# Four chained layers on one Trainium2 core: the second normalisation's transposes taken from TensorE to VectorE squares and DMA, and the last layer run two steps behind

## The chip, the core and the metric

The program runs on one core of one Trainium2 chip. The metric is the device time of the whole program in microseconds (us), median of the runs shown. The engines of the core run their own instruction streams side by side and wait for each other on semaphores: TensorE (PE in the rows, PEld its weight loads), VectorE (DVE), ScalarE (ACT), GpSimd (POOL) and SyncE (SP, which here only issues DMAs).

## The reference

Four layers, each added to the running x, over 2 sequences of 2048 tokens with 512 features:

```python
x = x + L0(x)   # gates, exponential averages, LayerNorm
x = x + einsum('bti,bio->bto', x, W[cat]) + b                      # L1
h = relu(einsum('bsh,bha->bsa', x, w1) + b1)                        # L2: 512 -> 128 -> 512
y = x + einsum('bsa,bah->bsh', h, w2) + b2
x = x + (y - mean(y)) * rsqrt(var(y) + 1e-5) * gamma + beta
x = x + einsum('bnh,boh->bno', x, W3[subj]) + b3                    # L3
```

The change touches nothing of L0. It is about L1, L2 and L3, which the program runs in its second part.

## The kernel before

The tokens are cut into 8 blocks of 512 tokens (NBLK = 8, LAST = 7), 4 blocks to a sequence (PER_SEQ = 4). The first part, to about 475 us of the trace, computes L0 for all blocks and keeps its results in DRAM (n_scratch, xt_scratch). The second part runs one step for each block i, in which L1 and the first half of L2 are done for block i and the rest for block i-1.

Every fp32 product is made of three passes: the operands are split in a high and a low part (x_h and x_l, s_h and s_l, t_h and t_l), and high by high, low by high and high by low are added up in PSUM (L628 to L630). The parts are made by two engines: ScalarE writes the high one and VectorE subtracts it for the low one. Within a product the features lie on the partitions. LayerNorm needs tokens on the partitions. So a block changes its layout twice in a step:

- `xx_product` (L867) brings x2, the result of L1, to tokens with four 128x128 transposes (L635, `turn`) and adds the L2 product to it in PSUM bank pm[k], for the token tile k;
- VectorE takes the statistics (`norm2_stats`, L1659), GpSimd makes scale and shift (`norm_scale`), ScalarE and VectorE each normalise two of the four tiles into stage_a (L1273, L1669);
- `turn_n2` (L882) brings the normalised block n2 back to features with 16 more transposes, in the middle of the next step's L1 product;
- `x3_sum_part` (L1633) makes gamma * n2 + (x2 + beta) from PSUM, `x3_hi_part` (L1257) and `x3_lo_part` (L1642) split it into t_h and t_l, and the L3 product (`l3_tile`, L911) uses them in the same step. ScalarE had made x2 + beta into soma (`x2_beta`, L1251).

The order of a step on TensorE is: L1 chunk 0, half of chunk 1, turn_n2 of two chunks, the rest of chunk 1, half of chunk 2, turn_n2 of two chunks, the rest, chunk 3, (in steps 5 and 6 also four turns of the next L1 input, `turn_y`), L3 tile 0, the first L2 product (`w1_product`), L3 tiles 1 and 2, the four `xx_product`, L3 tile 3. L1, L3 and w1 chunks are 12 matmuls of 512 columns each. L1 chunks alternate between two PSUM banks, so chunk 2 waits until ScalarE and VectorE have read chunk 0, and chunk 3 until they have read chunk 1 (`l1_product`, L833).

SyncE loads the next block's inputs (`load_y`, L417) and stores each output tile from one of two buffers in x_tok (`store_out`, L427); `output` (L1652) on VectorE waits for the store that last used its buffer. Steps 2, 3, 5 and 6 run in loops, steps 1, 4 and 7 are written out.

## Time and profile before

| | us |
|---|---|
| median of 3 runs (lowest, highest) | 754.29 (753.92, 754.69) |
| the profiled execution | 753.31 |
| its span, first to last instruction | 751.4 |
| TensorE busy in the span | 742.9 |
| VectorE, ScalarE, GpSimd busy | 536.7, 364.8, 113.2 |

The granted TensorE clock is 1.00 over the span. 1.9 us of the profiled execution lie outside the span, and the median is 1.0 us above that execution. Matmuls overlap in the rows: one of 512 columns is shown as 0.39 us long while the next begins 0.23 us after it, so what one costs is read from the distance of two beginnings.

### The profile page before, as it was taken

Reading aid. Unit: us, or ns where it says so; the run is one execution under the profiler, and the core shown is the slowest. Engines: PE = TensorE matmul, PEld = TensorE weight load, DVE = VectorE, ACT = ScalarE, POOL = GpSimd, SP = SyncE. Lnnn points to the kernel's source line nnn. Section 1 sums busy time; section 2 is a strip of 40 time slices with the busy share of each in tenths; the row PEclk is TensorE's granted clock in tenths of the full one; section 3 lists DMA queues with packets and bytes.
Section 4 is the critical chain, followed back from the end, with each engine's and each line's share of the span. In section 5 each row is a group of like instructions: output and inputs, shape, how many; then the busy total and the mean of one; then the engine's idle time right before and its main releaser. Section 6 shows DMA issues by size and latency. Waiting matters only on the chain.

```text
span 751.4 us, 10452 instructions
## 1 busy us (share of the span) xinstructions
PE 742.9 (99%) x3421; PEld 605.6 (81%) x3421; DVE 536.7 (71%) x790; ACT 364.8 (49%) x546; POOL 113.2 (15%) x222
## 2 busy tenths in 40 slices
PE   7999999999999999999999999999999999999997
PEld 6888888888888888788888788888888888888885
DVE  5598895695695595596587589866877767666645
ACT  4373346445436535535535543656563553635331
POOL 2000040030022013004004024124301021010110
PEclk9999999999999999999999999999999999999999
DMA  8863008916934953962971872526144131331002
GB/s 263 227 188 38 28 1 117 189 59 103 187 73 82 190 92 69 185 109 56 169 138 34 135 223 83 197 85 224 58 153 150 46 127 57 127 113 68 28 35 79
DMA packets 93068, 86.17 MB, mean 115 GB/s; under 512 B 61631, under 2 KB 75998, under 8 KB 90990
## 3 DMA queue, kind: packets, MB, share of 16 engines
q1 hardware_dynamic: 91662, 81.57, 45.4%
q10 hardware_dynamic: 1184, 4.23, 1.6%
q8 instruction: 15, 0.25, 0.1%
q0 software_dynamic: 192, 0.00, 0.1%
q14 instruction: 15, 0.12, 0.1%
HBM read 33.33 MB, written 25.20 MB: 78 GB/s over the span
## 4 chain that ended last, share of the span: by engine, by line
PE 98%; DVE 1%; DMA 0%; issue 0%; ACT 0%; DVEq 0%; ACTq 0%
PE pc L630 13%; PE pc L628 13%; PE pc L629 13%; PE pm L628 6%; PE pm L629 6%; PE pm L630 6%; PE pt L628 6%; PE pt L630 6%; PE pt L629 6%; PE pm L747 4%; PE pm L746 4%; PE pm L745 4%; PE pm L635 3%; PE pt L635 3%; PE pm L877 1%; PE pm L878 1%
## 5 line engine op out<-in xcount | busy, mean ns | idle before, releaser
L628 PE MATMUL pc<-x_h,wg_h 128*128 128x512 f32 x224 | 88.5, 395 | 0.1
L630 PE MATMUL pc<-x_h,wg_l 128*128 128x512 f32 x224 | 88.0, 393 | 0.0
L629 PE MATMUL pc<-x_l,wg_h 128*128 128x512 f32 x224 | 87.7, 391 | 0.0
L1443 DVE TENSOR_TENSOR_SCAN stage_b<-alpha,carry,stage_b 128x512 f32<-128x512 f32 x64 | 78.4, 1267 | 0.0
L628 PE MATMUL pm<-wo_h,s_h 128*128 128x512 f32 x128 | 50.7, 396 | 0.0
L1119 ACT ACTIVATE ctx_t<-ctx_t,col_all 128x512 f32<-128x512 f32 x32 | 23.1, 723 | 56.6 <-DVE ctx_t L1423 56.6
L630 PE MATMUL pm<-wo_h,s_l 128*128 128x512 f32 x128 | 50.5, 395 | 0.0
L629 PE MATMUL pm<-wo_l,s_h 128*128 128x512 f32 x128 | 50.5, 395 | 0.0
L747 PE MATMUL pm<-t_h,wt_l 128*128 128x512 f32 x128 | 50.5, 395 | 0.0
L746 PE MATMUL pm<-t_l,wt_h 128*128 128x512 f32 x128 | 50.4, 394 | 0.0
L745 PE MATMUL pm<-t_h,wt_h 128*128 128x512 f32 x128 | 50.4, 394 | 0.0
L628 PEld LDWEIGHTS pc<-x_h,wg_h 128*128 128x128 f32 x224 | 42.1, 188 | 10.2 <-issue 1.2
L630 PEld LDWEIGHTS pc<-x_h,wg_l 128*128 128x128 f32 x224 | 42.1, 188 | 9.3
L629 PEld LDWEIGHTS pc<-x_l,wg_h 128*128 128x128 f32 x224 | 42.1, 188 | 9.1
L1396 DVE SCALAR_TENSOR_TENSOR gate<-gate,soma 128x512 f32<-128x512 f32 x32 | 21.9, 697 | 36.7 <-ACT gate L1074 36.6
L522 POOL TENSOR_TENSOR newton<-mv,const 128x4 f32<-128x4 f32 x16 | 9.6, 600 | 251.0 <-DVE mv L1664 180.9
L1437 DVE SCALAR_TENSOR_TENSOR stage_b<-mod,w_blend,ctx_t 128x512 f32<-128x512 f32 x64 | 45.6, 754 | 2.4 <-DVE ctx_t L1427 1.5
L1074 ACT ACTIVATE gate<-pm,col_all 128x512 f32<-128x512 f32 x32 | 21.6, 688 | 45.4 <-PE pm L747 30.9
L1125 ACT ACTIVATE t_h<-stage_b 128x512 fp32r<-128x512 f32 x32 | 20.4, 637 | 47.5 <-DVE stage_b L1450 47.4
L1273 ACT ACTIVATE stage_a<-pm,nbias,rstd 128x512 f32<-128x512 f32 x16 | 11.6, 774 | 55.9 <-POOL nbias L538 55.8
L1630 DVE SCALAR_TENSOR_TENSOR s_l<-pc,seq_b,s_h 128x512 fp32r<-128x512 f32 x28 | 21.0, 750 | 24.0 <-ACT x_t L1248 24.0
L630 PE MATMUL pc<-x_h,ws_l 128*128 128x512 f32 x96 | 38.0, 395 | 0.0
(248 smaller groups left out, 1932.3 us busy)
## 6 DMA issues: line engine op xcount, KB each, us to landing
x_planes<-x_pairs SPq DMA_DIRECT2D x52, 256.0 KB, 7.4
xt_scratch<-x_t SPq DMA_DIRECT2D x8, 1024.0 KB, 10.2
n_scratch<-stage_a SPq DMA_DIRECT2D x8, 1024.0 KB, 10.1
ctx_t<-xt_scratch SPq DMA_DIRECT2D x16, 512.0 KB, 6.6
x_pairs<-n_scratch SPq DMA_DIRECT2D x14, 512.0 KB, 5.3
out_dram<-x_tok SPq DMA_DIRECT2D x28, 256.0 KB, 2.0
mod<-mod_scratch ACTq DMA_DIRECT2D x8, 512.0 KB, 3.6
stage_b<-in_L_cond_weight_dram SPq DMA_DIRECT2D x2, 1024.0 KB, 5.6
```

Source lines behind the costliest of these rows:

```text
L628: nc.tensor.matmul(acc, ah, bh, start=start and q == 0, stop=False)
L629: nc.tensor.matmul(acc, ah, bl, start=False, stop=False)
L630: last = nc.tensor.matmul(acc, al, bh, start=False, stop=stop and q == n - 1)
L635: last = nc.tensor.matmul(acc[:, q * P:(q + 1) * P], src, ident[:, :], is_transpose=True, start=(q == 0), stop=stop and (q == 3), skip_gro ...
L745: nc.tensor.matmul(pm[m][:, :], wt_h[:, c, o], t_h[:, c, :], start=(c == 0), stop=False)
L746: nc.tensor.matmul(pm[m][:, :], wt_h[:, c, o], t_l[:, c, :], start=False, stop=False)
L747: last = nc.tensor.matmul(pm[m][:, :], wt_l[:, c, o], t_h[:, c, :], start=False, stop=(c == NC - 1))
L1074: nc.scalar.activation(gate[:, m % 2, :], pm[m][:, :], ACT.Tanh, bias=cols["btemp"][:, m:m + 1], scale=0.5).then_inc(gate_t, 1)
L1119: nc.scalar.activation(ctx_t[:, m, :], ctx_t[:, m, :], ACT.Tanh, bias=cols["bg"][:, m:m + 1], scale=0.5).then_inc(z_t, 1)
L1396: nc.vector.scalar_tensor_tensor(gate[:, m % 2, :], gate[:, m % 2, :], 1.0, soma[:, m, :], ALU.add, ALU.mult).then_inc(s_prod, 1)
L1437: nc.vector.scalar_tensor_tensor(tr[:, m % 2, :], mod[:, d, :], w_blend[:, d, m:m + 1], ctx_t[:, m, :], ALU.mult, ALU.mult).then_inc(prods, 1)
L1443: nc.vector.tensor_tensor_scan(tr[:, m % 2, :], alpha[:, 1 + d:2 + d].to_broadcast([P, BLK]), tr[:, m % 2, :], carry[:, D - d, m:m + 1], A ...
```

## The change

- For blocks 1 to 6 TensorE no longer turns n2. ScalarE normalises all four tiles (not two), VectorE transposes each tile in squares of 32x32 (`turn_squares`) from stage_a into stage_b, and 16 DMAs of 32 partitions and 64 KB each (`move_square`) put the squares where a full transpose has them, in x_planes. ScalarE multiplies by gamma and adds beta while it copies them back to stage_b (`scale_n2`), and `x3_sum_part` adds x2. Blocks 0 and 7 are still turned by TensorE.
- Move issues are SyncE's, except that in blocks 1 and 6 six of the 16 are ScalarE's.
- The L3 product of block j is done in step j+2 and no longer in step j+1. So x2 is kept for a step longer, in x_t and soma by turns, and x2_beta is gone. x3_hi, x3_lo and L3 of block 6 come behind step 7.
- Step 1 has only two L3 tiles, step 2 the other two of block 0. The four turns of the second L3 weight (`turn_l3`) stand around the first and last two xx_products of step 1. Step 3 has its splits in another order on ScalarE and VectorE.
- The second L2 weights are loaded to gate, and VectorE makes their low parts. SyncE issues the loads of blocks 2 and 3 in step 1 and those of block 4 behind the moves of block 1; the later loads stand between the stores of a step, behind its moves. All loops of the second part are written out.

```diff
+        def x2_of(i):
+            return x_t if i % 2 == 0 else soma
+        def x3_parts_of(j):
+            return (s_h, s_l) if j == LAST - 1 else (t_h, t_l)
+        def turned_by_pe(j):
+            return j == 0 or j == LAST
+        def n2_acts(j):
+            return 2 + 4 * j - (2 if j == LAST else 0)
+        squares = stage_b[:, :, :].rearrange("p a e -> p (a e)").rearrange("p (f k i) -> p f k i", k=TILES, i=32)
+        squares_q = stage_b[:, :, :].rearrange("p a e -> p (a e)").rearrange("p (c q r) -> p c q r", c=NC, q=4)
+        def x3_of(j):
+            return x_planes if turned_by_pe(j) else stage_b
...
+        def move_square(engine, q, a):
+            part, tok = slice(32 * a, 32 * a + 32), slice(P * a, P * a + P)
+            engine.dma_start(x_planes[32 * q:32 * q + 32, :, tok], squares_q[part, :, q, :]).then_inc(n2_in, 16)
+        BY_ACT = [(q, a) for q in (2, 3) for a in range(1, 4)]
+        def shares_moves(j):
+            return j == 1 or j == LAST - 1
...
+            def move_n2(j):
+                sp.wait_ge(n2_squares, j * TILES)
+                if j == 1:
+                    sp.wait_ge(x3_lo, NC)
+                else:
+                    sp.wait_ge(n2_scaled, (j - 1) * NC)
+                for q in range(4):
+                    for a in range(4):
+                        if not (shares_moves(j) and (q, a) in BY_ACT):
+                            move_square(sp, q, a)
...
+            for i in range(2, NBLK):
+                move_n2(i - 1)
+                if i == 2:
+                    load_y(4)
+                    store_out(0, 2)
+                    store_out(0, 3)
+                    continue
+                store_out(i - 2, 0)
+                store_out(i - 2, 1)
+                if i + 2 < NBLK:
+                    load_y(i + 2)
+                store_out(i - 2, 2)
+                store_out(i - 2, 3)
+            for j in (LAST - 1, LAST):
                 for k in range(TILES):
                     store_out(j, k)
...
+            def l3_tile(j, k):
+                b = j // PER_SEQ
+                if turns_y(j + 2) and k < 3:
+                    pe.wait_ge(n2_act, n2_acts(j + 1))
+                elif turns_y(j + 2):
+                    pe.wait_ge(y_sum, (j + 3) * NC + 3)
+                elif j == LAST - 1 and k >= 2:
+                    pe.wait_ge(n2_act, n2_acts(LAST))
+                    pe.wait_ge(n2_dve, 4)
+                elif j == LAST - 1 and k == 0:
+                    pe.wait_ge(out_ready, j * TILES - 1)
+                else:
+                    after(pe, out_ready, j * TILES + max(k - 1, 0))
+                ch, cl = x3_parts_of(j)
+                for c in range(NC):
+                    if k == 0:
+                        pe.wait_ge(x3_hi, j * NC + c + 1)
+                        pe.wait_ge(x3_lo, j * NC + c + 1)
+                    last = product(l3_bank(j, k)[:, :], [(ch[:, c, tok], cl[:, c, tok], wh[:, c, :], wl[:, c, :])],
+                                   start=(c == 0), stop=(c == NC - 1))
+                last.then_inc(l3_mm, 1)
...
+            def last_blocks():
+                l3_tile(LAST - 1, 0)
+                l3_tile(LAST - 1, 1)
+                turn_n2(LAST)
+                l3_tile(LAST - 1, 2)
+                l3_tile(LAST - 1, 3)
...
+            def scale_n2(j, m):
+                b = j // PER_SEQ
+                act.wait_ge(n2_in, j * 256)
+                nc.scalar.activation(stage_b[:, m, :].rearrange("p (k a i) -> p k a i", k=TILES, a=4),
+                                     x_planes[:, m, :].rearrange("p (a k i) -> p k a i", k=TILES, a=4), ACT.Identity,
+                                     bias=seq["beta_b2"][:, b, m:m + 1],
+                                     scale=seq["gamma2"][:, b, m:m + 1]).then_inc(n2_scaled, 1)
...
+            def turn_squares(j, k):
+                dve.wait_ge(n2_act, n2_acts(j - 1) + k + 1)
+                if j == 1:
+                    dve.wait_ge(l3_turned, 2 * NC)
+                else:
+                    dve.wait_ge(x3_lo, j * NC)
+                nc.vector.transpose(squares[:, :, k, :], stage_a[:, k, :].rearrange("p (f i) -> p f i", i=32)
+                                    ).then_inc(n2_squares, 1)
...
+            def x3_sum_part(j, m):
+                dve.wait_ge(x2_hi, j * NC + (m + 1))
+                if turned_by_pe(j):
+                    dve.wait_ge(tn_done, (0 if j == 0 else NC) + (m + 1))
+                    after(dve, n2_scaled, 0 if j == 0 else (LAST - 1) * NC)
+                    nc.vector.scalar_tensor_tensor(x_planes[:, m, :], n2_bank(j, m)[:, :],
+                                                   seq["gamma2"][:, j // PER_SEQ, m:m + 1], x2_of(j)[:, m, :],
+                                                   ALU.mult, ALU.add).then_inc(x3_sum, 1)
+                else:
+                    dve.wait_ge(n2_scaled, (j - 1) * NC + (m + 1))
+                    nc.vector.tensor_tensor(stage_b[:, m, :], stage_b[:, m, :], x2_of(j)[:, m, :],
+                                            ALU.add).then_inc(x3_sum, 1)
```

The TensorE order at the end of the program, before: the last L3 tile of block 6, then `turn_n2(LAST)` and the L3 product of block 7.

```order
L630 MATMUL pt<-wt_h,t_l 128x512
L635 MATMUL pc<-ident,stage_a 128x128 [waits n2_dve,n2_act]
L635 MATMUL pc<-ident,stage_a 128x128 x7
L635 MATMUL pt<-ident,stage_a 128x128 [waits out_ready]
L635 MATMUL pt<-ident,stage_a 128x128 x3
L635 MATMUL pt<-ident,stage_a 128x128 [waits out_ready]
L635 MATMUL pt<-ident,stage_a 128x128 x3
L978 MATMUL pm<-wt_h,t_h 128x512 [waits x3_lo,x3_hi]
```

The same place after the change; L682 is `turn`, L675 to L677 are the three passes of `product`, and s_h and s_l are the parts of block 6.

```order
L677 MATMUL pt<-wt_h,s_l 128x512
L682 MATMUL pc<-ident,stage_a 128x128 [waits n2_dve,n2_act]
L682 MATMUL pc<-ident,stage_a 128x128 x7
L682 MATMUL pm<-ident,stage_a 128x128 x8
L675 MATMUL pm<-wt_h,s_h 128x512 [waits n2_dve,n2_act]
```

All four L3 tiles of block 6 come behind step 7 now: two ahead of the turns, two between them and the L3 product of block 7.

VectorE at the beginning of a step in the loop of steps 2 and 3, before: x2_lo (L1630), x3_sum (L1639) and x3_lo (L1645) of the block before, by turns.

```order
L1630 SCALAR_TENSOR_TENSOR s_l<-pc,seq_b,s_h 128x512 [waits x2_hi]
L1634 ISA
L1639 SCALAR_TENSOR_TENSOR gate<-pt,seq_gamma,soma 128x512 [waits x2_all,tn_done]
L1634 REGISTER_ALU
L1639 SCALAR_TENSOR_TENSOR gate<-pt,seq_gamma,soma 128x512 [waits x2_all,tn_done]
L1645 TENSOR_TENSOR t_l<-gate,t_h 128x512 [waits x3_hi,l3_mm] x2
L1628 REGISTER_ALU [waits w1_mm]
L1630 SCALAR_TENSOR_TENSOR s_l<-pc,seq_b,s_h 128x512 [waits x2_hi]
```

VectorE from the end of step 2 into step 3 after the change: x3_sum (L1714) of block 1, then x2_lo (L1700) of block 3, x3_lo (L1727) of block 1, the squares (L1761) of block 2 and y_sum (L1545) of block 4.

```order
L1746 BN_AGGR mv<-stats 128x2 [waits ln2_stats]
L1714 TENSOR_TENSOR stage_b<-stage_b,soma 128x512 [waits n2_scaled,x2_hi] x4
L1700 SCALAR_TENSOR_TENSOR s_l<-pc,seq_b,s_h 128x512 [waits x2_hi,w1_mm]
L1727 TENSOR_TENSOR t_l<-stage_b,t_h 128x512 [waits x3_hi,l3_mm] x4
L1761 STREAM_TRANSPOSE stage_b<-stage_a 128x16x32 [waits x3_lo,n2_act]
L1545 SCALAR_TENSOR_TENSOR ctx_t<-x_pairs,col_all,ctx_t 128x512 [waits yn_in,yx_in]
L1700 SCALAR_TENSOR_TENSOR s_l<-pc,seq_b,s_h 128x512 [waits x2_hi,w1_mm]
```

Between the x2_lo of chunk 0 and that of chunk 1 two x3_lo stood before; now all four, a square transpose and a y_sum stand there.

## Rows read from the trace of the kernel before

**Rows 1.** The page: busy time by engine, and the chain that ended last

```profile
PE 742.9 (99%) x3421; PEld 605.6 (81%) x3421; DVE 536.7 (71%) x790; ACT 364.8 (49%) x546; POOL 113.2 (15%) x222
PE 98%; DVE 1%; DMA 0%; issue 0%; ACT 0%; DVEq 0%; ACTq 0%
```

**Rows 2.** Timeline of PE, step 3: start, length, line, tiles, shape, count

```profile
573.25 0.40 PE L628 MATMUL pc<-x_h,wg_h 128*128 128x512 f32 x1
...
577.16 0.39 PE L630 MATMUL pc<-x_h,wg_l 128*128 128x512 f32 x1
577.39 1.03 PE L635 MATMUL pt<-ident,stage_a 128*128 128x128 f32 x8
578.18 0.48 PE L628 MATMUL pc<-x_h,wg_h 128*128 128x512 f32 x1
578.50 0.39 PE L629 MATMUL pc<-x_l,wg_h 128*128 128x512 f32 x1
...
604.59 0.40 PE L628 MATMUL pc<-x_h,wo_h 128*128 128x512 f32 x1
```

**Rows 3.** Timeline of PE, the end of the program

```profile
733.14 0.39 PE L630 MATMUL pt<-wt_h,t_l 128*128 128x512 f32 x1
733.63 1.06 PE L635 MATMUL pc<-ident,stage_a 128*128 128x128 f32 x8
734.53 1.04 PE L635 MATMUL pt<-ident,stage_a 128*128 128x128 f32 x8
736.72 0.47 PE L978 MATMUL pm<-wt_h,t_h 128*128 128x512 f32 x1 [1.14 <-DVE t_l L1645]
...
747.76 0.40 PE L980 MATMUL pm<-wt_h,t_l 128*128 128x512 f32 x1
```

**Rows 4.** Groups by line and form: busy us, mean ns | idle before

```profile
L1645 DVE TENSOR_TENSOR t_l<-gate,t_h 128x512 fp32r<-128x512 f32 x32 | 22.2, 713 | 2.0 <-ACT t_h L1260 1.1
L1623 DVE SCALAR_TENSOR_TENSOR x_l<-ctx_t,col_all,x_h 128x512 fp32r<-128x512 f32 x32 | 23.3, 760 | 1.4
L1443 DVE TENSOR_TENSOR_SCAN stage_b<-alpha,carry,stage_b 128x512 f32<-128x512 f32 x64 | 78.4, 1267 | 0.0
L1248 ACT ACTIVATE x_t<-pc,seq_b1b 128x512 f32<-128x512 f32 x32 | 21.8, 680 | 0.4 <-PE pm L879 0.4
L1260 ACT ACTIVATE t_h<-gate 128x512 fp32r<-128x512 f32 x32 | 20.2, 633 | 23.3 <-DVE gate L1639 22.9
L1273 ACT ACTIVATE stage_a<-pm,nbias,rstd 128x512 f32<-128x512 f32 x16 | 11.6, 774 | 55.9 <-POOL nbias L538 55.8
```

**Rows 5.** Timelines of VectorE, GpSimd and ScalarE, statistics to normalisation, step 2

```profile
571.49 0.18 DVE L1664 BATCH_NORM_AGGREGATE mv<-stats 128x2 f32<-128x6 f32 x1
...
571.75 0.20 POOL L522 TENSOR_TENSOR newton<-mv,const 128x4 f32<-128x4 f32 x1 [28.82 <-DVE mv L1664]
...
574.63 1.45 ACT L1273 ACTIVATE stage_a<-pm,nbias,rstd 128x512 f32<-128x512 f32 x2 [8.62 <-POOL nbias L538]
```

**Rows 6.** Timelines, step 1: its first PE row, GpSimd's identity add

```profile
511.30 0.40 PE L628 MATMUL pc<-x_h,wg_h 128*128 128x512 f32 x1
...
526.42 3.35 POOL L563 TENSOR_TENSOR stage_b<-stage_b,ident 128x128 f32<-128x128 f32 x4 [5.74 <-DMA stage_b<-in_L_cond_weight_dram]
```

**Rows 7.** DMA issues by line (ns min/median/max) and landing; DMA view, 299.5 to 307.5 us

```profile
L302 SPq DMA_DIRECT2D x_planes<-x_pairs x52: 603/622/1763, 22.9 to 418.0; - x52
DMA to landing us min/median/max: 4.4/7.4/10.2
L429 SPq DMA_DIRECT2D out_dram<-x_tok x28: 332/338/366, 530.1 to 734.3; - x28
L1115 ACTq DMA_DIRECT2D mod<-mod_scratch x8: 345/351/357, 27.0 to 430.8; - x8
...
DMA packets 1088, 1.15 MB, mean 144 GB/s; under 512 B 63, under 2 KB 1074, under 8 KB 1074
q1 hardware_dynamic: 1088, 1.15, 121.4%
```

## What the change was predicted to do, before it was run

> **What bounds the kernel now.** I read the page first: TensorE is busy for 742.9 of 751.4 us, and the chain that ended last is TensorE's for 98% [rows 1]. So time can only be won by taking work from TensorE or by closing its pauses, and it is lost where TensorE newly waits. Next I read TensorE's timeline of one step for what a turn costs [rows 2], then its end of the program, where its last pauses are [rows 3]. The groups by form give what VectorE and ScalarE pay for one 128x512 operation [rows 4], the three timelines of rows 5 the way from statistics to normalised tiles, and the DMA rows what moves inside SBUF cost [rows 7]. The step from 573.25 to 604.59 is 31.34 us long and has no pause in it [rows 2].
>
> **Term 1, the turns that leave.** The matmul before the turn begins at 577.16 and the second one behind it at 578.50, 1.34 us later; two ordinary distances are 0.46 us. Eight transposes cost 0.88 us, a block's sixteen 1.76 us, and six blocks 10.6 us [rows 2]. They lie on the path that sets the end. Products, xx_products and the turns of blocks 0 and 7 stay. A step of 31.34 us becomes 29.6.
>
> **Term 2, the end.** The last L3 tile of block 6 is issued until 733.37 (733.14 + 0.23), sixteen transposes would end at 735.13, and the next product begins at 736.72: 1.6 us of pauses [rows 3]. After the change two L3 tiles (24 matmuls, 5.6 us) stand between the turns and that product, so its wait for x3 goes. What is late next are the statistics of block 7, since VectorE now does x3 of block 6 ahead of them. Counted from the start of step 7: the squares of block 6 are ready at about 11.2 (L1 chunk 3 is being made until 11.0), the moves take 9.3 us (term 4), so they land at 20.5; four scalings and four high parts on ScalarE (eight at 0.63 to 0.68, 5.2 us) end at 25.7, the last low part at 26.4, four statistics with their aggregates at about 1.0 each at 30.4, GpSimd takes 3.0 (571.67 to 574.63) and the two normalisations 1.45 [rows 4, 5]: 34.9. TensorE is at the turns at 29.6 + 5.6 = 35.2. With some ten handings-over between engines, estimated at 0.1 each, a pause of about 0.7 is left: gain 0.9. From the product at 736.72 on, nothing changes (14.7 us to the end of the span).
>
> **Term 3, step 3.** Here the order of VectorE's work makes a new wait. I count from the first matmul of step 3. Before, the last statistics ended 1.2 us after the last xx_product (the aggregate ends at 571.67, the xx_products at 573.25 - 2.80 for an L3 tile = 570.45) [rows 2, 5]. After the change step 3 begins straight behind the xx_products of step 2, so x3_sum of block 1 starts at 1.2 and its four additions end at 4.0 (0.69 each [rows 4]). ScalarE's copy of x2 waits for all four: 4.7. Its low part ends at 5.4, and L1 chunk 2 needs it at 5.5 (24 matmuls at 0.23): just in time. Chunk 3 needs the low part of chunk 1 at 8.3. But in front of it stand: x3_hi of chunks 0 and 1 (to 6.0), ScalarE's two copies of x2 chunk 1 (to 7.3), x3_hi 2 and 3 (to 8.6), VectorE's last x3_lo (9.3), a square (10.0), y_sum (10.7), and the low part itself (11.4). With operations overlapping at their ends, as L1645 does in groups, it is 10.9. So TensorE waits 2.6 to 3.1 us; I take 2.7. In later steps all x3 work is done before chunk 0 is finished (four high parts end at 2.8, chunk 0 at 2.9), the low part of chunk 1 comes at 7.6, and nothing waits.
>
> **Term 4, the moves.** A block's 16 DMAs move 1.05 MB. The trace has no such DMA. The nearest are the four DMAs of 256 KB from x_pairs to x_planes, also inside SBUF, to 64 partitions, in pieces of 1 KB: issues of 0.62 us, landing 7.4 us after the issue, so 9.3 us from the first issue to the last landing for the same bytes [rows 7]. The new pieces are half as long. Lower bound: the issues, 16 at 0.34 (the store's 128 pieces [rows 7]) and 2 us behind, 7.4 us. Upper bound: a piece costs what one of 1 KB does; 1088 packets took 16 engines 8.0 us, 118 ns each, so 2048 would take 15.1 and with issue and landing 16.9 us [rows 7]. I take 9.3, since both carry the same bytes. What it may take: in a step of 29.6 us the squares are ready at 11.5. The moves land at 20.8, the store of output tile 0 is queued behind them and lands at 22.8, output tile 2 waits for its buffer (23.5), the statistics follow (27.1), x3_sum (29.9). It may be 32.5 before the next step's chunks suffer: the limit is 11.9 us, and at the seam, where x3_sum of block 1 has to end at 4.0 of step 3, it is about 12.5. ScalarE's own issues cost it six times 0.35 us [rows 7] in two steps in which it otherwise waits. Cost: 0, with 2.6 us of cover.
>
> The Trainium skill (SBUF, Door 1: The DMA port swizzle) says that 32 partitions reach only 8 of 16 ports and measured 189 GB/s there for 1 MiB. By it alone the data would take 5.5 us and the issues would bound the moves at 7.4, which takes another 0.5 us off the end. The row of DMAs to 64 partitions, 144 GB/s, is below what that page gives for 64 partitions (196), so I keep the row.
>
> **Term 5, the rest.** VectorE gains four squares and loses two normalisations, ScalarE the reverse and four scalings for four x2_beta. A square is an operation of 512 columns: at least 0.69, at most the 1.27 of a scan [rows 4]; I take 0.69. VectorE then works some 24 us of a step of 29.6, and at 1.27 some 26. It adds 0.6 us to term 3 and 1 us elsewhere if it is 1.27. In step 1 TensorE comes to turn_l3 one L3 tile earlier, at 529.9 (511.30 plus 18.6 us of work), and the weights are ready at 529.77 [rows 6]: no pause, with 0.2 us to spare and 0.3 at risk. The second L2 step has one L3 tile (2.8 us) to cover relu and its split, some 2.3 us: 0, or 0.3 if late.
>
> **Sum.** -10.6 - 0.9 + 2.7 = -8.8 us. Span 742.6, its execution 744.5, and against the median 754.29 the forecast is 745.5 us.
>
> **The rivals.**
> A, no new wait in step 3: if x3_sum of block 1 can start earlier or the order costs less than I count, only terms 1 and 2 act: 754.29 - 10.6 - 0.9 to 1.6, 742.1 to 743. For it: the other engines have much free time [rows 1]. Against it: the semaphores leave no other order.
> B, the moves are somewhat late, through slow squares, or since the loads of block 4 run beside ScalarE's last three moves: 12 to 12.9 us in all. Each microsecond over the limit is paid in five steps and once more at the end: 748 to 752.8.
> C, slower: each 512-byte piece costs nearly as much as one of 1 KB. Then the transfer takes the place of the turns as the bound, in every step: 5 x (m - 11.9) + (m - 9.3) us for moves of m us. It breaks even at 13.0 us and at 16.9 costs 33 - 8.8 = 24 us: up to 778. For it: the whole DMA time of the nearest row may be a price per piece, since no row holds the same bytes in other pieces. Against it: nothing shows such a price.
> The Trainium skill (DMA: Bandwidth & Descriptors, Why small descriptors are slow (HBM only)) says that transfers inside SBUF don't suffer from small pieces; by that C falls. No row here shows it.
> D, the change doesn't win what it takes off: TensorE's instructions go, but it waits as long elsewhere. The chain [rows 1] speaks against it.
>
> **How the numbers follow.** Forecast (744.5 to 748) 0.50; A 0.18; B 0.17; within 0.2% of before (D, or C at its break-even) 0.04; C 0.11. 0.2%, 1.5 us, is about what a measurement of this kernel tells from no change. Faster: 0.85, same 0.04, slower 0.11. The range of 8 in 10 goes from 742.5, just inside A, to 752.5, the end of B; A's lower edge, C and the rest, under 2 in 10, are left out.
>
> **What would show it.** TensorE's rows: steps 4 and 7 of 29.6 us; in step 3 a wait of 2.7 us before L1 chunk 3, put down to VectorE's s_l. Before turn_n2 of block 7 less than 1 us, before the last product none. The moves' last landing 9 to 10 us after the first issue; squares of 0.7 us on VectorE. If moves take over 12 us, TensorE waits in every step and rival C holds. If the wait in step 3 is missing, term 3 is wrong and A holds.

## The result: faster by 0.55%, less than half of the forecast

The changed kernel takes 751.19 us (median of 5 runs, 748.55 to 751.28); the kernel before, run beside it, 754.36 us (5 runs, 753.92 to 755.04). The ratio over all runs is 0.9945, with a 95% interval of 0.9930 to 0.9961: 3 to 5 us faster (the medians lie 3.2 apart), where 8.8 had been forecast. The time lies in the range and on the side that had 0.85, and 5.7 us above the forecast of 745.5.

The page of the changed kernel, where rows 1 have TensorE at 742.9 us and 3421 matmuls:

```profile
span 749.5 us, 10094 instructions
PE 737.3 (98%) x3325; PEld 599.2 (80%) x3325; DVE 538.6 (72%) x804; ACT 368.5 (49%) x550; POOL 123.6 (16%) x220
PEclk9999999999999999999999999999998999999999
```

The 96 transposes are gone, which by term 1 is 10.6 us, but TensorE is busy for 5.6 us less, not 10.6: most of the difference are matmuls that take longer, in step 3 and at the very start (both below). One of the 40 slices shows a granted clock below full speed; the page of before has none. The chain of waits of this profile breaks off early (its shares sum to 30% of the span), so I went by TensorE's timeline and by landmarks.

Three stretches of TensorE's timeline hold nearly all of it. First, step 4 of the changed kernel, beside rows 2 (start, length, operation):

```profile
599.79 0.40 PE L675 MATMUL pc<-x_h,wo_h 128*128 128x512 f32 x1
...
629.35 0.40 PE L675 MATMUL pc<-x_h,wo_h 128*128 128x512 f32 x1
```

29.56 us from the first product of one step to that of the next, where before had 31.34. The turns leave 1.78 us, as forecast. Then step 3, L1 chunk 3, with VectorE's rows of the same time, and TensorE's windows (busy us and count, granted clock, DMA share, GB/s):

```profile
572.26 0.40 PE L677 MATMUL pc<-x_h,wg_l 128*128 128x512 f32 x1
575.74 0.76 PE L675 MATMUL pc<-x_h,wg_h 128*128 128x512 f32 x1 [3.09 <-DVE s_l L1700]
576.31 0.63 PE L676 MATMUL pc<-x_l,wg_h 128*128 128x512 f32 x1
...
581.00 0.63 PE L675 MATMUL pt<-wg_h,t_h 128*128 128x512 f32 x1
```

```profile
569.44 1.28 DVE L1727 TENSOR_TENSOR t_l<-stage_b,t_h 128x512 fp32r<-128x512 f32 x2
572.19 1.29 DVE L1727 TENSOR_TENSOR t_l<-stage_b,t_h 128x512 fp32r<-128x512 f32 x2 [1.47 <-ACT t_h L1302]
573.59 0.71 DVE L1761 STREAM_TRANSPOSE stage_b<-stage_a 128x512 f32<-128x512 f32 x1
574.23 0.71 DVE L1545 SCALAR_TENSOR_TENSOR ctx_t<-x_pairs,col_all,ctx_t 128x512 f32<-128x512 f32 x1
574.85 0.75 DVE L1700 SCALAR_TENSOR_TENSOR s_l<-pc,seq_b,s_h 128x512 fp32r<-128x512 f32 x1
```

```profile
570.00:575.00 5.00, 2.66 (x12) 0.97 0.01 2
575.00:580.00 5.00, 4.26 (x10) 0.50 0.00 0
580.00:585.00 5.00, 5.00 (x20) 0.85 0.45 92
```

The wait is the one that term 3 built up link by link: two pairs of x3_lo, a square, a y_sum, then the low part that chunk 3 needs. From start to start it is 3.48 us where 0.23 is usual, so 3.2 us are lost. What no term had is behind it: the granted clock is 0.50 in the next window, the 1.2 GHz level, and the twelve matmuls of chunk 3 take 5.26 us (575.74 to 581.00) instead of 2.75. With a slow thirteenth that is another 2.7 us. Step 3 takes 35.55 us instead of 29.6.

Third, the seam, L3 tile (0,0) in step 1:

```profile
528.05 0.40 PE L677 MATMUL pt<-wg_h,t_l 128*128 128x512 f32 x1
529.54 0.47 PE L675 MATMUL pt<-wg_h,t_h 128*128 128x512 f32 x1 [1.09 <-DVE t_l L1723]
```

1.3 us of pause (1.49 between starts), for which the forecast had nothing. The tail went better than forecast: from step 7 on TensorE's timeline has no pause, in place of the 1.6 us of rows 3.

Two measures serve below. A **step** is the time from its first L1 product to that of the next step. The **path** is the time from the first product of step 1 (511.30 in rows 6, 513.72 in the changed kernel) to the start of the last matmul (747.76 in rows 3, 745.83). It is 236.46 us before and 232.11 after, so the change itself took 4.35 us off this path. Nearly all of the rest of the two profiles' difference lies at the very start, where nothing was changed: the first product of the gates begins at 12.07 us before and at 14.12 after. Experiment e11 looks at that.

### The profile page after: what moved, and what is told of

Its sections match the earlier page's. It is cut to its first block and busy times, and to the rows that moved or that the text cites. A ratio compares the mean times of both kernels' runs of the same rounds, so it can differ in the third digit from the quotient of the medians.

```text
span 749.5 us, 10094 instructions
## 1 busy us (share of the span) xinstructions
PE 737.3 (98%) x3325; PEld 599.2 (80%) x3325; DVE 538.6 (72%) x804; ACT 368.5 (49%) x550; POOL 123.6 (16%) x220
## 3 DMA queue, kind: packets, MB, share of 16 engines
HBM read 33.33 MB, written 25.20 MB: 78 GB/s over the span
## 5 line engine op out<-in xcount | busy, mean ns | idle before, releaser
L675 PE MATMUL pc<-x_h,wg_h 128*128 128x512 f32 x224 | 89.4, 399 | 3.2 <-DVE s_l L1700 3.1
L677 PE MATMUL pc<-x_h,wg_l 128*128 128x512 f32 x224 | 89.1, 398 | 0.0
L675 PEld LDWEIGHTS pc<-x_h,wg_h 128*128 128x128 f32 x224 | 42.7, 190 | 14.1 <-ACT soma L1292 3.5
L675 PE MATMUL pm<-wo_h,s_h 128*128 128x512 f32 x128 | 50.7, 396 | 0.0
L677 PE MATMUL pm<-wo_h,s_l 128*128 128x512 f32 x128 | 50.5, 395 | 0.0
L577 POOL TENSOR_TENSOR newton<-mv,const 128x4 f32<-128x4 f32 x16 | 11.6, 724 | 235.5 <-DVE mv L1746 163.8
L677 PEld LDWEIGHTS pc<-x_h,wg_l 128*128 128x128 f32 x224 | 42.7, 191 | 9.6
L677 PE MATMUL pc<-x_h,ws_l 128*128 128x512 f32 x96 | 38.0, 396 | 0.0
L675 PE MATMUL pt<-x_h,wg_h 128*128 128x512 f32 x96 | 37.9, 395 | 0.0
L675 PE MATMUL pc<-x_h,ws_h 128*128 128x512 f32 x96 | 37.9, 395 | 0.0
```

The costliest lines, as they stand in the source:

```text
L675: nc.tensor.matmul(acc, ah, bh, start=start and q == 0, stop=False)
L677: last = nc.tensor.matmul(acc, al, bh, start=False, stop=stop and q == n - 1)
```

## Experiments

Every kernel ran beside the kernel before, which took 754.1 to 754.8 us. The table has the median, the start of the gates' first product, steps 1 to 4, and the path. Then come the edits one by one.

| kernel | us | gates at | step 1 | step 2 | step 3 | step 4 | path |
|---|---|---|---|---|---|---|---|
| before | 754.3 | 12.07 | 30.56 | 31.39 | 31.34 | 31.34 | 236.46 |
| changed | 751.2 | 14.12 | 26.40 | 24.12 | 35.55 | 29.56 | 232.11 |
| e1_early | 749.9 | 13.65 | 26.39 | 23.96 | 30.69 | 34.50 | 231.98 |
| e2_half | 749.4 | 13.33 | 26.41 | 24.11 | 31.45 | 33.29 | 231.32 |
| e3_seam | 747.6 | 12.92 | 25.30 | 23.96 | 33.20 | 30.59 | 229.51 |
| e4_both | 747.5 | 13.07 | 25.30 | 23.96 | 30.59 | 33.17 | 229.17 |
| e5_share | 743.3 | 13.19 | 25.31 | 23.95 | 30.36 | 29.83 | 225.51 |
| e6_stores | 744.1 | 13.64 | 25.30 | 23.95 | 30.23 | 30.01 | 225.54 |
| e7_nomoves | 743.4 | 13.83 | 25.28 | 23.96 | 29.95 | 29.56 | 224.81 |
| e8_noturns | 750.3 | 14.18 | 30.55 | 30.48 | 30.45 | 30.77 | 231.81 |
| e9_share_only | 748.5 | 14.16 | 26.39 | 23.96 | 33.22 | 29.56 | 229.19 |
| e10_rows | 748.9 | 13.82 | 25.30 | 24.12 | 33.33 | 31.03 | 230.24 |
| e11_again | 754.0 | 12.85 | 30.56 | 31.38 | 31.34 | 31.35 | 236.45 |
| e12_all_sp | 751.5 | 12.59 | 26.40 | 24.12 | 34.42 | 29.56 | 233.49 |

The steps and the path of one kernel come from one execution each; those of the kernel before agree to 0.01 us in two. The times spread more: the changed kernel's five runs by 2.7 us, e1's seven by 5.0 (746.38 to 751.41). Each ratio to before has a 95% interval 0.3 to 0.4% wide, some 2.5 to 3 us. So a difference of 1 or 2 us between two of the medians shows nothing by itself, and what follows rests on steps and paths. Only e5, e6 and e7 (ratios 0.9856 to 0.9865) are clear of the changed kernel and of all the others.

### e1_early and e2_half: is it the order on VectorE?

e1, in VectorE's step2:

```
                     for m in range(NC):
+                        if j == 1 and m == 2:
+                            x2_lo_part(i, 1)
                         x3_lo_part(j, m)
...
-                x2_lo_part(i, 1)
+                if j != 1:
+                    x2_lo_part(i, 1)
```

> The changed kernel with one order altered in step 3: VectorE does x2_lo(3,1) after the second x3_lo of block 1, so ahead of two x3_lo, the square and y_sum. Theory (the pause of 3.24 us before L1 chunk 3 of step 3, and behind it 5.26 us of L1 at the lower granted clock, 2.75 us longer than at the full one, are one cause): both leave, step 3 goes from 35.6 to 29.6 us between its first product and that of step 4, granted clock 1.00 all through, and the time falls by 5 to 6 us against the changed kernel, to about 745.5 (747.5 if the start of the program is as late as in the changed kernel's profile). Rival (the lower clock comes from something else in this place): step 3 keeps a stretch at the lower clock, 32.3 us, time about 748. Second rival (the wait only moves, to x3_lo(1,2) and (1,3) and what follows): step 3 stays above 33 us.

The wait left its place: step 3 takes 30.69 us, with a pause of 0.86 us. But the median fell by 1.3 us only, which the spread doesn't tell from nothing, and the path by 0.1, since step 4 became 34.50 us, with a wait of the same name and size:

```profile
603.03 0.47 PE L675 MATMUL pc<-x_h,wo_h 128*128 128x512 f32 x1 [3.11 <-DVE s_l L1700]
```

e2 moves the same low part less far:

```
+                if j == 1:
+                    x2_lo_part(i, 1)
                 turn_squares(i - 1, 0)
                 if more and not turned:
                     y_sum_part(i + 1, 0)
-                x2_lo_part(i, 1)
+                if j != 1:
+                    x2_lo_part(i, 1)
```

> The changed kernel with x2_lo(3,1) of step 3 ahead of the square and the y_sum only, still behind all four x3_lo: the pause before L1 chunk 3 should shrink from 3.24 us by 1.26 to 1.3 us (rows: square 0.64, y_sum 0.62 from start to start), to about 1.9 us. If any pause of this size brings the lower clock, step 3 takes about 34.2 us and the time is about 1.3 us under the changed kernel's. If the clock falls only behind the longer pause, step 3 takes about 31.5 us and the time falls by 4 us.

The pause in step 3 went from 3.09 to 1.63 us, as counted from the rows, and step 3 took 31.45 us: no lower clock there. But step 4 then had a pause of 1.92 us, and that one with a stretch at the lower clock behind it. Steps 3 and 4 together take 65.11 us in the changed kernel, 65.19 in e1 and 64.74 in e2, where two free steps would take 59.1. So what I expected of e1 did not hold; the second rival came nearest, only that the wait moved a step on and not within step 3. The order in step 3 makes the wait there, and behind it stands a second hold that takes over when the first is removed. e2's step 3 came out as its second theory said (31.5 us), its time did not.

### e3_seam: the seam's pause

```
             normalise(0, 3)
-            y_sum_part(2, 2)
-            y_sum_part(2, 3)
             x2_lo_part(1, 2)
...
             x3_lo_part(0, 3)
+            y_sum_part(2, 2)
+            y_sum_part(2, 3)
```

> The changed kernel with y_sum(2,2) and y_sum(2,3) of VectorE behind the last x3_lo of block 0 instead of beside GpSimd's wo_l. Theory (the pause of 1.2 us in L3 tile (0,0), before its third chunk, comes from these two additions, 3.04 us beside GpSimd's subtraction where they take 1.40 by themselves): the pair takes 1.4 us, GpSimd's four subtractions 5.1 instead of 6.0, the pause in tile (0,0) goes, step 1 takes 25.2 instead of 26.4 us, time 1.0 to 1.3 us under the changed kernel's. Rival (something later in the seam is due next, y_hi or y_lo of block 2 before L1 of step 2): step 1 stays within 0.5 us of 26.4.

Step 1 took 25.30 us, 1.1 us less, and 0.38 us of pause is left. The rows show the price of two engines at work in SBUF at once. In the changed kernel, the pair of additions and GpSimd's subtraction beside it:

```profile
520.19 3.04 DVE L1545 SCALAR_TENSOR_TENSOR ctx_t<-x_pairs,col_all,ctx_t 128x512 f32<-128x512 f32 x2
...
518.41 5.98 POOL L629 TENSOR_TENSOR wo_l<-stage_b,wo_h 128x512 fp32r<-128x512 f32 x4
```

And in e3, with the pair moved:

```profile
527.49 1.61 DVE L1545 SCALAR_TENSOR_TENSOR ctx_t<-x_pairs,col_all,ctx_t 128x512 f32<-128x512 f32 x2
...
517.02 5.08 POOL L629 TENSOR_TENSOR wo_l<-stage_b,wo_h 128x512 fp32r<-128x512 f32 x4
```

The pair costs 1.4 us more and GpSimd's four subtractions 0.9 us more when they meet. The same four take 5.09 us in the kernel before, where no such pair stands beside them. The Trainium skill (SBUF — State Buffer, Who interferes with whom) says that an instruction of VectorE with two inputs in SBUF contends with one of GpSimd that reads SBUF, and that the one issued second waits for the first to finish. The rows agree: both sides got longer where they met. In e3 the pair runs beside four small additions of GpSimd (128x128, 527.65 to 531.16) and takes 1.61 us, where such a pair with GpSimd idle takes 1.41 (at 575.51 in the changed kernel). The median fell by more than expected (3.6 us; the intervals of the two kernels just overlap). Of the path's 2.6 us, 1.1 are step 1 and 1.3 steps 3 and 4, whose pauses (0.41, 2.71 and 0.78 us) had no stretch at the lower clock in this execution.

### e4_both: do they add?

> Both edits, of step 3 and of the seam, in one kernel. Theory (they are separate places on TensorE's path): their gains add, 6 us from step 3 and 1.2 from the seam against the changed kernel's profile, time about 744.3 to 746.5, and steps 1 and 3 take 25.2 and 29.6 us. Rival (the seam's gain is eaten up in step 2 or 3): the time of the kernel with step 3's edit alone.

They don't: 747.53 us is e3's time. Step 3 is free but for 0.76 us, and step 4 has the wait of e1 again, 3.35 us, this time at the full clock. SyncE's and VectorE's rows in step 3 of e4 name the second hold (the step began at 561.87):

```profile
577.17 11.28 SPq L303 DMA_DIRECT2D x_planes<-stage_b  x16
588.50 1.08 SPq L466 DMA_DIRECT2D out_dram<-x_tok  x2
...
590.90 0.69 DVE L1738 TENSOR_TENSOR x_tok<-pt,mod 128x512 f32<-128x512 f32 x1 [7.71 <-DMA out_dram<-x_tok]
591.51 0.69 DVE L1743 BATCH_NORM_STATS2 stats<-pm 128x6 f32<-128x512 f32 x1
...
600.60 0.74 DVE L1700 SCALAR_TENSOR_TENSOR s_l<-pc,seq_b,s_h 128x512 fp32r<-128x512 f32 x1
```

Sixteen issues take SyncE 11.3 us. The two stores stand behind them, output tile 2 waits 7.71 us for its buffer, and everything VectorE has to do until the low part for step 4 (statistics, x3_sum, x3_lo) is queued behind that tile.

### e5_share and e6_stores: which end of SyncE's queue counts?

Both start from e4. e5 gives ScalarE six moves in every block:

```
         def shares_moves(j):
-            return j == 1 or j == LAST - 1
+            return True
...
-                if i == 2:
-                    move_shares(1, BY_ACT[3:])
+                if i < LAST:
+                    move_shares(i - 1, BY_ACT[3:])
```

> The kernel with both edits (step 3, seam), and in it ScalarE issues six of a block's sixteen moves in every block, not in blocks 1 and 6 alone, three ahead of the relu and three behind it; so SyncE issues ten. Theory (the pause has gone from step 3 to step 4 because SyncE's sixteen moves, 0.70 us each instead of the 0.34 I took, and the two stores behind them hold up block 2's second pair of output tiles, the statistics behind these on VectorE, and so x2_lo(4,0)): SyncE's run of moves falls from 11.3 to about 7 us, output(1,2) comes 4 us sooner, the pause of 3.35 us in step 4 and its stretch at the lower clock go, step 4 takes 29.6 instead of 33.2 us, time about 743.5 (3.6 to 4 us under the kernel with both edits, 747.5). Rival (VectorE's own work, 25 instructions of 0.7 us a step, is the limit): step 4 stays at 33 us whoever issues.

e6 lets all sixteen stay with SyncE in blocks 2 to 5 and puts the stores between them:

```
                             move_square(sp, q, a)
+                            n += 1
+                            if n == 9 and 2 <= j < LAST - 1:
+                                store_out(j - 1, 0)
+                                store_out(j - 1, 1)
...
-                store_out(i - 2, 0)
-                store_out(i - 2, 1)
+                if i == LAST:
+                    store_out(i - 2, 0)
+                    store_out(i - 2, 1)
```

> The kernel with both edits, and in it SyncE issues the two stores of a block's first output tiles behind nine of the sixteen moves (blocks 2 to 5) instead of behind all sixteen; the moves themselves end 1.1 us later. Theory A (the stores behind the moves are what comes last in step 4): output(1,2) is done 5 us sooner, the statistics with it, but the scaled squares come 1.1 us later and are next; the pause in step 4 falls from 3.35 to about 1.5 us or less, time about 2 to 4 us under 747.5. Theory B (the landing of the moves comes last): the pause grows by 1 us and the time with it.

e5 takes 743.26 us, ratio 0.9856 (0.9840 to 0.9873): 4.3 us under e4. The wait of step 4 is gone:

```profile
576.73 8.04 SPq L303 DMA_DIRECT2D x_planes<-stage_b  x10
...
577.43 2.13 ACTq L303 DMA_DIRECT2D x_planes<-stage_b  x3
...
587.22 0.69 DVE L1738 TENSOR_TENSOR x_tok<-pt,mod 128x512 f32<-128x512 f32 x1 [4.42 <-DMA out_dram<-x_tok]
```

Ten issues take 8.0 us, where I had expected 7, and output tile 2 comes 10.5 us after the first move instead of 13.7. e6 takes 744.11 us, ratio 0.9865 (0.9849 to 0.9882), though block 2's squares are scaled 0.9 us later behind the first move than in e4 (13.7 against 12.8): its pause in step 4 is 0.24 us. So it was the stores behind the moves that held VectorE up, not the landing of the moves (theory A; theory B wanted more time). Its gain of 3.4 us is within the 2 to 4 that I had for A.

### e7_nomoves: what the moves cost in all

```
-                for q in range(4):
-                    for a in range(4):
-                        if not (shares_moves(j) and (q, a) in BY_ACT):
-                            move_square(sp, q, a)
...
-                act.wait_ge(n2_in, j * 256)
+                act.wait_ge(n2_squares, j * TILES)
...
-                for q, a in parts:
-                    move_square(act, q, a)
```

> The kernel with both edits and all 96 moves left out: ScalarE scales what stands in x_planes from before, so blocks 1 to 6 of the output lack their n2. It measures what the moves cost in all. Theory (moves and their issue are all that delays steps 3 to 5): steps 3 and 4 take 29.6 us each, no pause behind step 1's, time 741.5 to 743.5. Rival (VectorE's queue is late without any move too): a pause of over 1 us stays in step 3 or 4, time 746 or more.

743.42 us, e5's time. Step 4 takes 29.56, step 3 29.95 us, and no pause of over 0.3 us stands behind step 1's. Against e5, the 96 moves now cost 0.7 us of path. The rival, that VectorE's own work is the limit, is out.

### e8_noturns: the first term by itself

```
+                    if first_block(j) or last_block(j):
                         turn(n2_bank(j, c), [...]).then_inc(tn_done, 1)
+                    else:
+                        pe.sem_inc(tn_done, 1)
```

> The kernel before with the 96 transposes of n2 in blocks 1 to 6 left out and nothing put in their place (x3 of these blocks is made from what stands in the PSUM banks). It measures the first term of my sum by itself: 96 transposes, 1.76 us a block, are 10.6 us. Theory: steps 3 and 4 take 29.6 instead of 31.3 us, time 743.7 (10.6 under before). Rival (TensorE then waits for VectorE's work in each step, which it has hidden so far): less than 8 us come off, and pauses of over 0.3 us a step show.

The rival was right here: 3.8 us came off, not 10.6. In the old order a step without turns takes 30.5 to 30.8 us, for TensorE then waits for VectorE's low part once a step:

```profile
554.16 0.47 PE L628 MATMUL pc<-x_h,wg_h 128*128 128x512 f32 x1 [0.56 <-DVE s_l L1633]
584.60 0.47 PE L628 MATMUL pc<-x_h,wg_h 128*128 128x512 f32 x1 [0.66 <-DVE s_l L1633]
615.32 0.47 PE L628 MATMUL pc<-x_h,wo_h 128*128 128x512 f32 x1 [0.93 <-DVE s_l L1633]
```

The turns had been hiding VectorE's x3 work between the chunks of L1. In the changed kernel, with L3 two steps back and VectorE's work in another order, step 4 takes 29.56 us. So leaving out the turns doesn't bring in the 1.78 us without the rest of the change; which part of the rest is needed no run separates.

### e9_share_only: the second hold without the first

The edit of e5 on the changed kernel itself.

> The changed kernel with one part altered: ScalarE issues six of the sixteen moves in every block. Step 3 and the seam stay as the change has them. Theory (two holds stand one behind the other: the order on VectorE in step 3, and behind it SyncE's sixteen moves in step 4, so that either edit by itself is eaten up by the other hold): block 1's moves are shared already, so the pause of 3.1 us in step 3 stays, and step 4 had none; steps 3 and 4 take 33 to 35.6 and 29.6 us, the time is that of the changed kernel within 1 us, 749 to 751. Rival (the sharing helps by itself, through stores and loads that come sooner): 747.5 or less.

748.54 us (748.20 to 752.25), between my two numbers; its interval (0.9914 to 0.9958) overlaps the changed kernel's. The pauses of step 3 are as large as before (0.43 and 2.72 us), step 4 is free, and nothing of the lower clock shows in this execution: that is the 2.3 us by which step 3 is shorter. In the changed kernel's profile, step 3 was so late by its pause and the slow stretch that it covered the second hold.

### e10_rows: what sets the price of a move

On e4, each move carries 32 pieces of 2 KB instead of 128 of 512 B:

```
-                engine.dma_start(x_planes[32 * q:32 * q + 32, :, tok], squares_q[part, :, q, :]).then_inc(n2_in, 16)
+                engine.dma_start(x_planes[32 * q:32 * q + 32, a, :], stage_b[part, q, :]).then_inc(n2_in, 16)
```

> The kernel with the edits of step 3 and the seam (SyncE issues all sixteen moves in blocks 2 to 5), and each move carries the same 64 KB as 32 pieces of 2 KB, one a partition, instead of 128 pieces of 512 B; what is moved is then not n2's squares but rows of the same tile, so blocks 1 to 6 of the output are wrong by that. It measures what sets a move's issue at 0.70 us. If the pieces set it: the issue falls to 0.35 us or less, sixteen take under 6 us, the pause of 3.35 us in step 4 goes, time about 743.5 as with the shared moves. If the tiles in SBUF at both ends or the bytes set it: the issue stays near 0.70 us, the pause stays, time about 747.5.

```profile
579.14 10.73 SPq L303 DMA_DIRECT2D x_planes<-stage_b  x16
```

Sixteen issues take 10.7 us, 0.67 each, against 11.3 and 0.70 in e4. Over the trains of blocks 2 to 5 it is 42.8 us against 43.3: a quarter of the pieces saves 1%. Nor do the bytes set it, since an issue of 256 KB in rows 7 takes 0.62 us. So here the issue is paid by the instruction. The stores, from SBUF to memory, take 0.34 (rows 7). What it is in a move inside SBUF that costs twice that is not shown. The pauses of this execution (1.93 us in step 3, at the lower clock behind it, 1.22 in step 4) sum to less than e4's 4.1, but the pause of step 4 didn't stay at 3.35 us as I had expected. The one in step 3 is longer because block 1's squares are scaled from 2.1 us into the step (564.76 - 562.67) instead of 0.9, and it covers the second hold in part. So the time, 748.9, says nothing more than that the hold is still there.

### e11_again and e12_all_sp

e11 is the kernel before, unchanged.

> The kernel before once more, unchanged, for a second profile of it. It tells whether the start is part of the change: the first product of the gates (in the profile of before at 12.07 us) came at 14.12 us in the changed kernel and at 12.9 to 14.2 us in the eight kernels since. If the start's place varies by chance, it comes anywhere from 12 to 14.2 us here; if the changed code delays it, at 12.1 us. The time is 753.5 to 755 us.

The start varies by itself: 12.85 us here, with the path the same to 0.01 us, and in e8, which has the code of before there, 14.18. In all profiles but before's and e12's, the two with the earliest start, TensorE waits 0.3 to 1.0 us for the second tile of x. And in all of them its first transposes stand about 0.22 us apart instead of 0.11, until some 7 us in before's profile and until 8 to 10 in the others, and in five (the changed kernel, e7 to e10) the first matmuls of 512 columns stand 0.43 us apart too, at the latest until 11.6. That is the pace of the lower clock, but the profile gives a granted clock of 1.00 there; why it is slow stays open. The changed kernel's 14.12 is near the late end of all fourteen and before's 12.07 is the earliest, so at least some of the 2.05 us between the two profiles is chance. The changed kernel and the ten made from it begin at 13.5 us in the mean, the three profiles with before's code at 12.07, 12.85 and 14.18; whether there is a small systematic part can't be told from these.

e12 undoes one part of the change:

```
         def shares_moves(j):
-            return j == 1 or j == LAST - 1
+            return False
...
-                if i == LAST:
-                    move_shares(i - 1, BY_ACT[3:])
                 relu_part(i)
-                if i == 2:
-                    move_shares(1, BY_ACT[3:])
```

> The changed kernel with the moves of blocks 1 and 6 issued by SyncE alone too (one part of the change undone). Theory (a move costs SyncE 0.70 us, so sixteen take 11.3 instead of 7 us and block 1's squares are scaled 4 us later): the statistics of step 2 end before x3_sum(1) can start, x2_lo(3,1) comes 2 to 4 us later, step 3 takes 38 to 40 instead of 35.6 us, block 6's moves cost nothing to 1 us, time 753 to 756. Rival (the moves are covered even so, as my prediction had it for 9.3 us): time within 1 us of the changed kernel's 751.2.

751.50 us, the time of the changed kernel, but not for the rival's reason. In block 1 the scaling starts 12.5 us after the first issue, with ScalarE's help 12.1 (564.04 - 551.9): help saves next to nothing there. Three of ScalarE's moves stand behind the relu and are issued from 557.86 to 559.99, and the scaling starts only 4.1 us after that (a move takes 2.1 us to land in the median of this profile, 4.7 at most). From 559.13 on SyncE issues the loads of block 4 beside them, and the DMA engines are 83% busy or more in every microsecond from 559 to 564. In e12 these loads come behind the moves, and the scaling starts 1.5 us after the last issue has ended. That the loads slow the moves is rival B's second reason; no run takes the loads away by themselves. In block 6, where all six are ahead of the relu, the scaling starts 11.8 us after the first issue without help and 7.9 with it, and the tail then has two pauses that the changed kernel doesn't have:

```profile
723.20 0.50 PE L675 MATMUL pt<-wt_h,s_h 128*128 128x512 f32 x1 [1.54 <-DVE x_tok L1734]
727.17 1.06 PE L682 MATMUL pc<-ident,stage_a 128*128 128x128 f32 x8 [0.90 <-DVE stage_a L1747]
```

So the place that I named was wrong: block 6 pays, not block 1. The path is 1.4 us longer than the changed kernel's, with 2.4 us of new pauses (2.8 from start to start), less 1.1 us in step 3, whose stretch at the lower clock was shorter, and 0.3 in step 5. The median is only 0.3 us longer, less than the 2 to 5 us expected.

## Why the prediction was right in direction and wrong in size

**Which steps failed.** Two terms of the sum are wrong in the profiled execution. Term 3 priced the wait of step 3 by its own length, 2.7 us; the step lost 6.0 us (35.55 - 29.56), 3.2 of them the wait and 2.7 the lower clock behind it. Term 5 put the seam at nothing; it cost 1.3 us. Term 4, "cost: 0, with 2.6 us of cover", is wrong as well: where the wait of step 3 is shortened, the moves make one of 3.1 to 3.4 us in step 4 (e1, e4). The changed kernel's profile hides that.

**Term 1, the turns: right in this kernel.** Step 4 takes 1.78 us less (forecast 1.76). But e8 shows that the reason given was half of it. I wrote that the turns lie on the path and so come off it. They do with the rest of the change; by themselves they give 3.8 us, the rest going into VectorE's low parts. I gave this (rival D) almost no chance because the chain of rows 1 is TensorE's; a chain tells who was last, not how near the next one is.

**Term 2, the end: too small.** I took 0.7 us of pause to be left before turn_n2 of block 7; none is. Block 6's squares are scaled 7.9 us after the first issue, not 9.3 as I had put the landing. The gain is the full 1.6 us of rows 3.

**Term 3, step 3: the wait right, its consequence missing.** Forecast 2.7 us before chunk 3, put down to s_l; measured 3.1 to 3.2. The low part of chunk 1 ended at 11.36 of the step (575.60 - 564.24), which is the 11.4 of the plain sum and not the 10.9 with overlaps. That TensorE's granted clock can fall to the lower level behind such a pause had no place in the sum: 2.7 us more. This is the largest part of what is missing from the forecast in the profiled execution. Without the stretch not all of it would be won back: e3's profile has the same two holds without it, and its steps 3 and 4 take 63.8 us, against 65.1 here and 61.8 by my sum. So 1.3 us hang on the slow stretch, and 2.0 of the 3.3 would be there without it, 1.0 of them the hold of term 4. Whether the stretch is a source of the spread (748.55 to 751.28 us against before's 753.92 to 755.04) is not shown: the granted clocks of the five runs, 0.997, 1.000, 0.998, 0.997 and 0.995 from the fastest to the slowest, don't follow their times.

**Term 4, the moves: wrong in price and limit, and hidden here.** I took 9.3 us from first issue to last landing, from four DMAs of 256 KB, "since both carry the same bytes". Bytes don't set it; the number of issues does. Between the first issue and the scaling it was 13.2 us in step 3 (579.41 to 592.57) and 12.2 in step 4:

```profile
579.41 11.64 SPq L303 DMA_DIRECT2D x_planes<-stage_b  x16
...
L303 SPq DMA_DIRECT2D x_planes<-stage_b x84: 591/601/1983, 551.9 to 709.4; - x84
DMA to landing us min/median/max: 2.1/2.1/4.7
```

Rows 7 had the price: 0.62 us for an issue inside SBUF, by sixteen, and 2 us to land are 12 us. I used that row for its landing and the store's 0.34 for the issues. The second error lies in the limit. 11.9 us holds for a step whose squares are ready at 11.5; in step 3, where x3 of block 1 stands in front of them, they are ready at 15.2 (579.41 - 564.24). The stores and output tile 2 were in my chain, at the right place, but 3.7 us too early for that step. So "cost 0, with 2.6 us of cover" was wrong where it counted. The profile of the changed kernel doesn't show it, since the wait of step 3 covers it; e1 and e4 do, and e5, e6 and e7 show that it goes when the issues are shared, the stores come sooner, or the moves leave. From step 4 on, where I would have charged an excess in every step, the squares were scaled 12.2, 12.8 and 11.8 us after the first issue, and only step 5 lost something, 0.4 us (31.70 against the 31.29 of step 6), with output tile 2 waiting for its store again. So the sign I had named (moves over 12 us, TensorE waits in every step, rival C holds) did not hold.

**Term 5, the rest: one part right, one missed.** A square takes 0.70 us, as taken (24 of them, beside 0.71 for L1645 in rows 4):

```profile
L1761 DVE STREAM_TRANSPOSE stage_b<-stage_a 128x512 f32<-128x512 f32 x24 | 16.2, 695 | 0.9 <-ACT stage_a L1329 0.8
```

At the seam I looked at turn_l3 and its weights, and not at VectorE's y_sum, which the change puts beside GpSimd's subtraction and ahead of the first x3_lo. That cost the pause of 1.3 us in tile (0,0), of which e3 takes back 1.1.

**The sum on the path.** Forecast -8.8, measured -4.35. Step 3 has 3.3 more than term 3 (2.7 the clock, the rest the wait and what lies around it), the seam 1.3, step 5 0.4, the end 0.7 less: 4.3 of 4.45 us. The profiled execution (751.28) lies 6.8 us above the 744.5 that the sum gave for it: these 4.45, and 2.4 ahead of step 1, of which 2.05 are the late start that e11 puts down to chance in part. Before's profiled execution lay 1.0 us under its median, the changed kernel's at it, so the medians differ from the forecast by 5.7.

**The rivals.** B (moves late by 12 to 12.9 us, 748 to 752.8) gave the right time and about the right size for the moves, but not the right bill: they cost 0.4 us in this kernel's profile. The agreement of the time is luck. B's own range doesn't follow from its rule either: by the formula of C, 12 to 12.9 us are 748.7 to 754.1. C's price per piece is refuted by e10. A's number, 742.1 to 743, is what e5 reaches, with both holds and the seam mended.

## A faster version

e5_share keeps the change and mends three places: x2_lo(3,1) between the pairs of x3_lo, y_sum(2,2) and (2,3) behind x3_lo(0,3), and six of sixteen moves issued by ScalarE in every block. It takes 743.26 us (742.99 to 743.42, 4 runs), 1.44% under before (95% interval 1.27 to 1.60) and about 7.9 us under the changed kernel. Its path is 225.51 us, 10.95 less than before's. Two pauses are left in it, 0.38 us at the seam and 0.48 us in step 3:

```profile
527.16 0.47 PE L675 MATMUL pt<-wg_h,t_h 128*128 128x512 f32 x1 [0.38 <-DVE t_l L1723]
567.86 0.47 PE L675 MATMUL pc<-x_h,wg_h 128*128 128x512 f32 x1 [0.48 <-DVE s_l L1700]
```

## What to carry to other kernels

Price a train of DMAs by its issues first: count the instructions on each queue, take the issue time from a row with the same kind of ends, and ask what is queued behind the train, not only when it lands. When a wait is forecast or found, check which hold stands next behind it, in the step where that hold is tightest and not in the steady step; here the edit that took a wait of 3 us out of step 3 was worth 0.1 us of path by itself and 0.3 on top of the seam's, until the hold behind it was gone too; the three edits together gave 6.6 us of path and 7.9 of time. And work hidden under a bound engine is not spare: take the bound engine's work away by itself, as e8 does, to see how much of it comes back.

## What the hardware showed that I had not expected

- A pause of TensorE can cost more than its length. The granted clock fell from 2.4 to 1.2 GHz behind pauses of 3.09 us (changed kernel), 3.11 (e1), 1.92 (e2), 1.93 (e10) and 2.82 us (e12), for 7 to 12 matmuls shown at 0.63 us, which take 0.43 us from start to start instead of 0.23: 1.6 to 2.7 us in all. It stayed up behind 3.35 (e4), 2.72 (e9), 2.71 (e3) and 1.63 us (e2), and behind all shorter ones of the second part. So the length of the pause doesn't decide it alone; what else does is open. The window of e4 that holds its pause of 3.35 us and what follows it:

```profile
600.00:605.00 5.00, 3.51 (x15) 1.00 0.00 0
605.00:610.00 5.00, 5.00 (x23) 1.00 0.13 26
```

- An issue of a DMA inside SBUF costs SyncE 0.60 us and the next begins after 0.63 to 0.73 (trains of 16 take 10.0 to 11.6 us), whether it has 32 pieces of 2 KB or 128 of 512 B, where a store of 128 pieces to memory costs 0.34. With ScalarE issuing moves beside it, SyncE's ten took 8.04 us in step 3 of e5, but 6.87 in that of e9; what makes the difference is not shown.
- VectorE's addition with all operands in SBUF took 1.52 us instead of 0.70 beside GpSimd's 128x512 subtraction (3.04 for two in the changed kernel, 1.41 for two with GpSimd idle).
